# Linear attention on one core: the order of the row normalisation and the rotary sums on VectorE

## The chip, the cores and the metric

The kernel runs on one core of a Trainium2 chip. The metric is the device time of one execution in microseconds. The kernel before took 2188.58 us (median of three runs, 2188.2 to 2190.31 us).

## The reference, cut to what matters

The reference is a block of three layers over x of shape (2, 2048, 256) in f32: softmax attention, linear attention, and a feed-forward net of coupled cycles that stands between the two and again behind them. The change touches the linear attention alone. For each batch it computes:

```
q = silu(x @ Wq);  k = silu(x @ Wk);  v = x @ Wv      # 16 heads of 16
q = rope(q);  k = rope(k)        # t * cos + rotated(t) * sin
energy = (q @ k.T) * lower_triangle
out = energy @ v
out = out * sigmoid(x @ Wg1 @ Wg2)
mu = mean(out);  var = mean((out - mu) ** 2)
out = (out - mu) / sqrt(var + 1e-5) * ln_w + ln_b
x = x + out @ Wo
```

## The kernel before, in words

The five engines run programs of their own and meet at semaphores (names such as `l_s`, `l_n`; a wait names the count it wants). The linear attention goes over 32 tiles of 128 tokens (16 to a batch). The causal sum over earlier tiles is carried in a state (`s_x`, 256 x 16 values of k.T @ v laid on a diagonal), so each tile needs its own 128 x 128 energies and the state of the tile before.

`through_tiles` calls an engine's `pipeline(n, p, place)` for n = 0 to 33 in order; p is n's parity and picks one of two buffers. Tiles 4 to 13 and 18 to 29 are visited in two hardware loops, two tiles to an iteration (5 and 6 iterations, so 4 and 5 jumps back); the others are written out. One visit n works on several tiles at once. On TensorE, in this order, with the lines of the matmuls:

- `energy(n)` L860, sixteen matmuls of 32 rows, q.T k for tile n; `rows(n-1)` L892, the attention output of tile n-1 turned back into rows
- `project_vg(n+1)` L840 (values and gate), `project_qk(n+2)` L831 (queries and keys), `turn(n+1)` L848 (rotated q and k turned)
- `attend(n)`: L873 (state times q), L879 (masked energies times v), and at its end L883, which multiplies the rotated keys `qk_r` by v into the next state and then raises `l_s`
- `out_proj(n-2)` L910, and last `norm_turn(n-1)` L900: two transposes of the normalised rows `o_n` of tile n-1, behind `l_n`

On VectorE a visit is `mask(n, 0..3)` L1457 with `gated(n-1)` L1475 and L1478 (gate, then row statistics) between the masks, `variance(n-1)` L1481 and L1483, `rope(n+2)`, `normalise(n-1)` L1488, `state(n)` L1468 and `residual(n-2)` L1493. `rope` is four products of q and k with cosines and sines into a buffer `rt` (L1445) and then a difference and a sum (L1450, L1451, the sums from here on) into `qk_r[p]`. The sums wait for `l_s` of tile n: `qk_r` has two buffers, and the one for tile n+2 is still read by L883 of tile n. `normalise(n-1)` waits for `l_rs`, the reciprocal root that GpSimd makes (`output_root`, L1622) from the variance, and for `l_y` of the tile before. ScalarE takes the silu (L1120), copies results out of PSUM (`turned`, L1135 to L1141; the attention output, L1162) and applies the layer norm's weights to the turned rows (`affine`, L1148).

In a visit n the tiles for which a step has nothing to do leave it out: `normalise` and `norm_turn` are there from n = 1 on, `rope` up to n = 29. The order on each engine is written by hand; nothing reorders it.

Of the kernel before, what the change touches and what calls it, by code (L numbers as in the profile page):

```python
# [67 lines left out]
def hybrid_block(nc, x, wq, bq, wk, bk, wv, bv, wo, bo, lq, lk, lv, lo, g1, g2, ln_w, ln_b,  # L68
                 c1, d1, c2, d2, c3, d3, c4, d4, e1, f1, e2, f2, e3, f3, ar,
                 ident_in, cos_in, sin_in, causal_in, head_in, diag_in, sign_in, out):  # L70
    with ExitStack() as ctx:
# [112 lines left out]
        def take(*shape, dt=F32):  # L184
            n = int(np.prod(shape))
            words = n if dt == F32 else n // 2
            ap = work[:, at[0]:at[0] + words]
            at[0] += words
            assert at[0] <= WORK, at[0]
            if dt != F32:  # L190
                ap = ap.bitcast(dt)
            names = "abcd"[:len(shape)]
            return ap.rearrange(f"p ({' '.join(names)}) -> p {' '.join(names)}", **dict(zip(names, shape)))
# [33 lines left out]
        qk_a, qk_r = take(2, 2 * DIM), take(2, 2 * DIM)  # L227
# [92 lines left out]
        def is_tile(m):  # L320

            return not isinstance(m, int) or 0 <= m < TILES
# [17 lines left out]
        def wait(eng, s, value):  # L340

            if not isinstance(value, int) or value > 0:
                eng.wait_ge(s, value)
# [841 lines left out]
        def _(dve):  # L1185
# [5 lines left out]
            def moments_of(st, c):  # L1191

                g = st * NCH + c
                wait(dve, n_mv, g - 1)
                for t in range(4):
                    m = dve.bn_stats(bn6[:, c % 2, t], X[:, 4 * c + t, :])
                m.then_inc(n_bn, 1)
                dve.wait_ge(n_bn, g + 1)
                wait(dve, n_rs, g - NCH + 1)
                if st == 3:  # L1200
                    dve.wait_ge(n_sh, c + 1)
                for t in range(4):
                    m = dve.bn_aggr(moments[:, c, t], bn6[:, c % 2, t])
                m.then_inc(n_mv, 1)
# [227 lines left out]
            def halves(ap):  # L1432
                v = ap.rearrange("p (h a e) -> p h a e", a=2, e=HD // 2)
                return v[:, :, 0, :], v[:, :, 1, :]

            def rope(n, p, t):

                dve.wait_ge(l_silu, n + 1)
                wait(dve, l_rope, n)
                a, b = halves(qk_a[:, p, :])  # L1440
                ra, rb = halves(qk_r[:, p, :])
                co = cos_s[:, bass.ds(t, 1), :].broadcast_to((P, 2 * HEADS, HD // 2))
                si = sin_s[:, bass.ds(t, 1), :].broadcast_to((P, 2 * HEADS, HD // 2))
                for i, (u, v) in enumerate(((a, co), (b, si), (b, co), (a, si))):
                    m = dve.tensor_tensor(rt[:, i], u, v, ALU.mult)  # L1445
                m.then_inc(l_rt, 1)
                dve.wait_ge(l_rt, n + 1)
                wait(dve, l_s, n - 1)
                wait(dve, l_t, n - 1)
                dve.tensor_tensor(ra, rt[:, 0], rt[:, 1], ALU.subtract)  # L1450
                dve.tensor_tensor(rb, rt[:, 2], rt[:, 3], ALU.add).then_inc(l_rope, 1)  # L1451

            def mask(n, i):
                dve.wait_ge(l_e, 4 * (n + 1))
                if i == 0:
                    wait(dve, l_o, n)
                dve.tensor_tensor(e_m[:, i], ps[:, 3 + i, :].rearrange("p (a n) -> p a n", n=P),  # L1457
                                  causal[:].rearrange("p (a n) -> p a n", a=1).broadcast_to((P, 2 * KT, P)),
                                  ALU.mult).then_inc(l_em, 1)

            def state(n, reset):

                dve.wait_ge(l_s, n + 1)
                dve.wait_ge(l_o, n + 1)
                if reset:
                    dve.memset(s_x, 0.0).then_inc(l_sx, 1)
                else:
                    dve.tensor_tensor(s_x.rearrange("p k n -> p (k n)"), ps[:, 2, 0:DIM],  # L1468
                                      diag[:].rearrange("p h d -> p (h d)"), ALU.mult).then_inc(l_sx, 1)

            def gated(n, p):

                dve.wait_ge(l_gate, n + 1)
                dve.wait_ge(l_ot, n + 1)
                dve.scalar_tensor_tensor(out=o_r[:, p, :], in0=gate[:, p, :], scalar=1.0, in1=ps[:, 0, 0:DIM],  # L1475
                                         op0=ALU.add, op1=ALU.mult).then_inc(l_r, 1)
                dve.wait_ge(l_r, n + 1)
                dve.bn_stats(stats[:], o_r[:, p, :]).then_inc(l_bn, 1)  # L1478

            def variance(n, p):  # L1480
                dve.bn_aggr(mv[:, p, :], stats[:]).then_inc(l_mv, 1)  # L1481
                dve.wait_ge(l_mv, n + 1)
                dve.tensor_scalar(var_e[:, p:p + 1], mv[:, p, 1:2], EPS, None, ALU.add).then_inc(l_ve, 1)  # L1483

            def normalise(n, p):
                wait(dve, l_y, n - 1)
                dve.wait_ge(l_rs, n + 1)
                dve.tensor_scalar(o_n[:, p, :], o_r[:, p, :], mv[:, p, 0:1], rstd[:, p:p + 1],  # L1488
                                  ALU.subtract, ALU.mult).then_inc(l_n, 1)

            def residual(n):
                dve.wait_ge(l_w, n + 1)
                dve.tensor_tensor(X[:, bass.ds(n, 1), :], X[:, bass.ds(n, 1), :],  # L1493
                                  ps[:, 1, 0:DIM].rearrange("p (a n) -> p a n", a=1), ALU.add).then_inc(l_x, 1)

            def pipeline(n, p, place):
                if is_tile(n):
                    mask(n, 0)
                    mask(n, 1)
                if is_tile(n - 1):  # L1500
                    gated(n - 1, 1 - p)
                if is_tile(n):
                    mask(n, 2)
                if is_tile(n - 1):
                    dve.wait_ge(l_bn, n)
                if is_tile(n):
                    mask(n, 3)
                if is_tile(n - 1):
                    variance(n - 1, 1 - p)
                if is_tile(n + 2):  # L1510
                    rope(n + 2, p, place)
                if is_tile(n - 1):
                    normalise(n - 1, 1 - p)
                if is_tile(n) and is_tile(n + 1):
                    state(n, isinstance(n, int) and n % TPB == TPB - 1)
                if is_tile(n - 2):
                    residual(n - 2)
                if isinstance(n, int) and n >= TILES - 2:
                    for c in ((0,), (1,), (2, 3), (4, 5))[n - TILES + 2]:
                        dve.wait_ge(l_x, 4 * (c + 1))  # L1520
                        moments_of(3, c)

            dve.tensor_reduce(parity[:, 0:1], head[:].rearrange("p (j a) -> p a j", a=2)[:, 0:1, :], AX_X, ALU.add).then_inc(l_par, 1)
            dve.tensor_reduce(parity[:, 1:2], head[:].rearrange("p (j a) -> p a j", a=2)[:, 1:2, :], AX_X, ALU.add).then_inc(l_par, 1)
            dve.memset(v_x, 0.0).then_inc(l_vz, 1)
            rope(0, 0, 0)
            rope(1, 1, 1)
            dve.memset(s_x, 0.0).then_inc(l_sx, 1)
            through_tiles(dve, pipeline)

            dve.wait_ge(l_x, TILES)
# [164 lines left out]
```

## Time and profile before

| | |
|---|---|
| three runs, median (range) | 2188.58 us (2188.2 to 2190.31) |
| profiled execution | 2187.72 us |
| its span on the core | 2185.9 us |
| busy: TensorE, VectorE, ScalarE, GpSimd | 96%, 81%, 68%, 6% |
| mean granted TensorE clock | 0.979 |

The span is the time from the first to the last instruction that the profiler saw; the execution's own time has 1.82 us more around it. Granted clock 1.00 is 2.4 GHz and 0.50 is 1.2 GHz. Softmax attention fills the span to about 1400 us, the first feed-forward net to about 1685 us, the linear attention about 1685 to 1990 us, the second feed-forward net the rest.

### The profile page before, as it was taken

To read this page: it belongs to the slowest core of one execution; us is meant where nothing else is said; L and a number is where in the kernel's file an instruction comes from. 1 tells how busy PE (TensorE), PEld (TensorE's weight loads), DVE (VectorE), ACT (ScalarE), POOL (GpSimd) and SP (SyncE) were. 2 spreads that over 40 slices of the span, in tenths; PEclk is the share of its full clock that TensorE was granted. 3 is DMA by queue.
4 is the path that set the end of the run, shared out by engine and by line. 5 is a ranking of instruction groups with operands and counts; after the bars stand their busy time and mean duration, and the time that the engine had idled before them with its cause. 6 is when DMAs were issued, how large, how long until landed. Compare 5 with 4: busy or idle time off the path is not lost.

```text
span 2185.9 us, 48580 instructions
## 1 busy us (share of the span) xinstructions
PE 2102.3 (96%) x14502; PEld 880.0 (40%) x14502; DVE 1774.6 (81%) x3326; ACT 1476.2 (68%) x2899; POOL 134.0 (6%) x210
## 2 busy tenths in 40 slices
PE   7799999999999999999999999899998999998998
PEld 4323333333333333333333333244336555554435
DVE  6789999999999999999999999653546777775344
ACT  3438888888888888888888888744556434346653
POOL 1340000000000000000000000010002000002000
PEclk9779999999999999999999999999999999998999
DMA  6421221221221221211211211230000000000002
GB/s 161 139 64 42 53 73 41 62 63 41 64 60 41 67 57 43 71 51 46 73 47 50 72 43 49 78 106 11 0 0 1 1 0 1 0 0 1 0 1 78
DMA packets 93689, 101.24 MB, mean 46 GB/s; under 512 B 35712, under 2 KB 74896, under 8 KB 93552
## 3 DMA queue, kind: packets, MB, share of 16 engines
q1 hardware_dynamic: 93552, 99.79, 16.3%
q8 instruction: 40, 0.66, 0.1%
q14 instruction: 97, 0.79, 0.1%
HBM read 78.72 MB, written 20.71 MB: 45 GB/s over the span
## 4 chain that ended last, share of the span: by engine, by line
PE 85%; DVE 4%; issue 4%; ACT 3%; SPq 3%; DMA 1%; ACTq 0%; POOL 0%; DVEq 0%; POOLq 0%
PE ps L617 22%; PE ps L592 14%; PE ps L640 10%; PE ps L646 10%; PE ps L752 8%; PE ps L760 4%; PE ps L831 2%; PE ps L840 2%; PE ps L860 2%; ACT YT L1019 1%; PE ps L606 1%; PE ps L773 1%; PE ps L879 1%; PE ps L821 1%; SPq L359 1%
## 5 line engine op out<-in xcount | busy, mean ns | idle before, releaser
L1305 DVE TENSOR_REDUCE mx<-ps 128x1 f32<-128x512 f32 x2048 | 1279.4, 683 | 20.7 <-PE ps L592 15.5
L1019 ACT ACTIVATE YT<-ps 128x512 f32<-128x512 f32 x2048 | 1058.0, 606 | 250.8 <-PE ps L646 250.7
L617 PE MATMUL ps<-YT,work 128*32 128x512 f32 x4096 | 546.1, 605 | 0.0
L592 PE MATMUL ps<-work 64*128 64x512 bf16 x2048 | 461.0, 389 | 12.5 <-DVE mx L1305 10.5
L640 PE MATMUL ps<-work 64*128 64x512 bf16 x2048 | 401.8, 378 | 1.7
L646 PE MATMUL ps<-work 34*128 34x512 bf16 x2048 | 398.4, 378 | 0.0
L592 PEld LDWEIGHTS ps<-work 64*128 64x128 bf16 x2048 | 144.6, 93 | 617.8 <-DVE mx L1305 544.8
L640 PEld LDWEIGHTS ps<-work 64*128 64x128 bf16 x2048 | 161.6, 94 | 106.1 <-ACT YT L1019 31.6
L752 PE MATMUL ps<-YT,c_s 128*128 128x512 f32 x384 | 180.4, 613 | 3.2 <-ACT work L1059 2.5
L617 PEld LDWEIGHTS ps<-YT,work 128*32 128x32 f32 x4096 | 80.7, 108 | 122.8 <-issue 86.9
L1059 ACT ACTIVATE work<-ps,bias 128x512 f32<-128x512 f32 x96 | 60.7, 683 | 90.4 <-PE ps L752 90.4
L646 PEld LDWEIGHTS ps<-work 34*128 34x128 bf16 x2048 | 101.0, 94 | 49.5 <-issue 1.3
L1457 DVE TENSOR_TENSOR work<-ps,causal 128x512 f32<-128x512 f32 x128 | 81.8, 682 | 37.0 <-PE ps L860 37.0
L752 PEld LDWEIGHTS ps<-YT,c_s 128*128 128x128 f32 x384 | 70.4, 193 | 94.7 <-issue 94.6
L1590 POOL COPY work<-vals 128x512 f32 (+1 forms) x32 | 19.6, 614 | 1191.8 <-PE ps L617 1191.7
L760 PE MATMUL ps<-work,c_s 128*128 128x512 f32 x192 | 90.2, 592 | 0.0
L1395 DVE TENSOR_TENSOR work<-work,YT 128x512 f32<-128x512 f32 x36 | 24.7, 687 | 68.6 <-ACT work L1083 68.5
L1148 ACT ACTIVATE work<-ps,bias 128x128 f32<-128x128 f32 x64 | 25.8, 453 | 59.5 <-PE ps L900 59.5
L1128 ACT ACTIVATE work<-ps 128x128 f32<-128x128 f32 x64 | 14.3, 275 | 76.2 <-PE ps L840 76.2
L831 PE MATMUL ps<-lqk_s,work 128*128 128x512 f32 x128 | 62.1, 607 | 1.9 <-ACT work L1120 1.9
L840 PE MATMUL ps<-lvg_s,work 128*128 128x512 f32 x128 | 60.3, 594 | 0.0
L1445 DVE TENSOR_TENSOR work<-work,cos_s 128x256 f32<-128x256 f32 x64 | 27.2, 425 | 35.5 <-ACT work L1120 35.5
(151 smaller groups left out, 1775.9 us busy)
## 6 DMA issues: line engine op xcount, KB each, us to landing
work<-k_scr SPq DMA_DIRECT2D x640, 64.0 KB, 2.1
work<-q_scr SPq DMA_DIRECT2D x640, 32.0 KB, 1.8
o_scr<-o_sb SPq DMA_DIRECT2D x32, 256.0 KB, 2.2
X<-in_L_attn_a_x_dram SPq DMA_DIRECT2D x8, 512.0 KB, 7.2
work<-negt SPq DMA_DIRECT2D x256, 1.0 KB
work<-o_scr SPq DMA_DIRECT2D x16, 256.0 KB
work<-inv_scr SPq DMA_DIRECT2D x16, 256.0 KB
out_dram<-X SPq DMA_DIRECT2D x16, 256.0 KB, 2.1
```

The source lines that it names most:

```text
L592: mm(ps[:, bank_of[x], :], qa[rows, p, jp, qt * P:(qt + 1) * P], ka[rows, p, kc_ * CH:(kc_ + 1) * CH], start=True, stop=True).then_inc(a_m ...
L617: m = mm(ps[32 * j:32 * j + 32, 7, :], vst[:, p, t, :], prob(GROUP * t + j), start=t == 0, stop=t == KTILES - 1)
L640: mm(ps[:, S_BANK + (u + g) % S_RING, :], kb[rows, p, t * P:(t + 1) * P], qb[rows, p, jp, :], start=True, stop=False)
L646: mm(ps[:, S_BANK + (u + g) % S_RING, :], kc[rows, p, t * P:(t + 1) * P], qc[rows, p, jp, :], start=False, stop=True).then_inc(qk_mm, 1)
L752: m = mm(ps[:, mt, :], c1_s[:, kt, mt * P:(mt + 1) * P], YT[:, kt, ch(c)], start=kt == 0, stop=kt == KT - 1)
L760: m = mm(ps[:, 2, :], c2_s[:, kt, :], h1[:, (c - 1) % 2, kt, :], start=kt == 0, stop=kt == KT - 1)
L831: m = mm(ps[:, 0, :], y_st8[:, p, kt, :], lqk_s[:, kt, :], start=kt == 0, stop=kt == KT - 1)
L840: m = mm(ps[:, 1, :], y_st8[:, p, kt, :], lvg_s[:, kt, :], start=kt == 0, stop=kt == KT - 1)
L1019: fn(prob(u), ps[:, S_BANK + u % S_RING, :], ACT.Exp, scale=HD ** -0.5).then_inc(exp_ok, 1)
L1059: m = fn(h1[:, c % 2, mt, :], ps[:, mt, :], ACT.Gelu, bias=bias[:, D1 + mt:D1 + mt + 1])
L1305: dve.tensor_reduce(mx[:, p, at_:at_ + 1], ps[:, bank_of[x], :], AX_X, ALU.max).then_inc(a_max, 1)
L1457: dve.tensor_tensor(e_m[:, i], ps[:, 3 + i, :].rearrange("p (a n) -> p a n", n=P), causal[:].rearrange("p (a n) -> p a n", a=1).broadcast_ ...
```

## The change

`rope` is cut into two functions, its four products and its two sums. In a visit, `normalise(n-1)` is issued behind the products of tile n+2 and ahead of its sums; before, it came behind the sums. The wait for the silu stays with the products; the waits for the products themselves, for `l_s` and for `l_t` go with the sums. Nothing is added or removed: the same instructions and waits are issued in another order on VectorE, and no other engine's program is touched.

```diff
-            def rope(n, p, t):
+            def rope_products(n, p, t):
 
                 dve.wait_ge(l_silu, n + 1)
                 wait(dve, l_rope, n)
                 a, b = halves(qk_a[:, p, :])
-                ra, rb = halves(qk_r[:, p, :])
...
                 for i, (u, v) in enumerate(((a, co), (b, si), (b, co), (a, si))):
                     m = dve.tensor_tensor(rt[:, i], u, v, ALU.mult)
                 m.then_inc(l_rt, 1)
+
+            def rope_sums(n, p):
+
+                ra, rb = halves(qk_r[:, p, :])
                 dve.wait_ge(l_rt, n + 1)
                 wait(dve, l_s, n - 1)
                 wait(dve, l_t, n - 1)
...
                 if is_tile(n + 2):
-                    rope(n + 2, p, place)
+                    rope_products(n + 2, p, place)
                 if is_tile(n - 1):
                     normalise(n - 1, 1 - p)
+                if is_tile(n + 2):
+                    rope_sums(n + 2, p)
                 if is_tile(n) and is_tile(n + 1):
                     state(n, isinstance(n, int) and n % TPB == TPB - 1)
...
-            rope(0, 0, 0)
-            rope(1, 1, 1)
+            for n in range(2):
+                rope_products(n, n, n)
+                rope_sums(n, n)
```

## Rows read from the trace of the kernel before

**Rows 1.** The page: busy time by engine.

```profile
PE 2102.3 (96%) x14502; PEld 880.0 (40%) x14502; DVE 1774.6 (81%) x3326; ACT 1476.2 (68%) x2899; POOL 134.0 (6%) x210
```

**Rows 2.** By stretch: busy PE, PEld, DVE, ACT, POOL; clock; DMA share; GB/s.

```profile
60.00:200.00 140.00, 125.24 (x628) 42.56 (x627) 123.51 (x208) 70.04 (x124) 42.26 (x19) 0.82 0.29 83
...
1690.00:1965.00 275.00, 261.37 (x2267) 159.67 (x2267) 196.37 (x502) 111.84 (x328) 25.81 (x58) 1.00 0.00 1
```

**Rows 3.** Who waited for whom on TensorE, 1685 to 1990 us.

```profile
PE ps L900 <- DVE work L1488: 13.8, 30, 2.2
PE ps L860 <- issue: 2.1, 9, 0.3
```

**Rows 4.** The chain that ended last, part of a tile: start, length, what.

```profile
1867.61 0.68 DVE work L1445 x2
1868.29 0.39 issue
```

**Rows 5.** Timeline, TensorE in one tile: start, length, engine, line.

```profile
1765.35 1.08 PE L879 MATMUL ps<-work 128*32 128x128 f32 x32
1766.36 0.71 PE L883 MATMUL ps<-work 128*128 128x128 f32 x4
1766.91 1.03 PE L910 MATMUL ps<-lo_s,work 128*128 128x256 f32 x4
1768.31 0.44 PE L900 MATMUL ps<-ident,work 128*128 128x128 f32 x2 [0.37 <-DVE work L1488]
1768.67 1.15 PE L860 MATMUL ps<-work 32*128 32x256 f32 x16
...
1770.03 1.88 PE L840 MATMUL ps<-lvg_s,work 128*128 128x512 f32 x4
1771.74 1.94 PE L831 MATMUL ps<-lqk_s,work 128*128 128x512 f32 x4
```

**Rows 6.** Timeline, VectorE and GpSimd in the same tile.

```profile
1764.44 0.54 POOL L1622 TENSOR_TENSOR rstd<-var_e,mhalf 128x1 f32<-128x1 f32 x1 [8.56 <-DVE var_e L1483]
...
1766.49 0.42 DVE L1445 TENSOR_TENSOR work<-work,sin_s 128x256 f32<-128x256 f32 x1
1767.16 0.42 DVE L1450 TENSOR_TENSOR work<-work 128x256 f32<-128x256 f32 x1 [0.26 <-DVE work L1445]
...
1767.84 0.41 DVE L1488 TENSOR_SCALAR work<-work,mv,rstd 128x256 f32<-128x256 f32 x1
...
1768.50 0.41 DVE L1493 TENSOR_TENSOR X<-X,ps 128x256 f32 x1
1769.96 1.29 DVE L1457 TENSOR_TENSOR work<-ps,causal 128x512 f32<-128x512 f32 x2 [1.05 <-PE ps L860]
1771.17 0.41 DVE L1475 SCALAR_TENSOR_TENSOR work<-work,ps 128x256 f32<-128x256 f32 x1
```

**Rows 7.** Timeline, TensorE in visit 30, which has no rotary products or sums.

```profile
1969.81 1.03 PE L910 MATMUL ps<-lo_s,work 128*128 128x256 f32 x4
1970.68 0.38 PE L900 MATMUL ps<-ident,work 128*128 128x128 f32 x2
1970.99 1.15 PE L860 MATMUL ps<-work 32*128 32x256 f32 x16
```

**Rows 8.** Timeline, visit 1, the first with a normalisation and without `out_proj`.

```profile
1701.29 0.42 DVE L1445 TENSOR_TENSOR work<-work,sin_s 128x256 f32<-128x256 f32 x1
...
1701.43 0.71 PE L883 MATMUL ps<-work 128*128 128x128 f32 x4
1703.38 0.44 PE L900 MATMUL ps<-ident,work 128*128 128x128 f32 x2 [1.24 <-DVE work L1488]
```

**Rows 9.** Timeline, TensorE where a loop jumps back.

```profile
1758.78 0.44 PE L900 MATMUL ps<-ident,work 128*128 128x128 f32 x2 [0.37 <-DVE work L1488]
1759.44 1.15 PE L860 MATMUL ps<-work 32*128 32x256 f32 x16 [0.23 <-issue]
```

**Rows 10.** Timeline, TensorE in visit 31, after the tiles touched.

```profile
1976.23 1.94 PE L879 MATMUL ps<-work 128*32 128x128 f32 x32 [3.28 <-DVE work L1457]
```

## The prediction

> **What bounds the kernel now.** I began with the page. TensorE is busy 96% of the span, VectorE 81% [rows 1]. Over the whole TensorE is the bound, but a change in the linear attention is worth what that stage allows, so the second view was the busy time by stretch: between 1690 and 1965 us TensorE is busy 261.37 of 275 us at clock 1.00, VectorE only 196.37 us, and the DMA share is nil [rows 2]. No throughput is missing there; TensorE stands still for 13.63 us in small gaps. The third view, who waited for whom, names them: most are the transposes of the normalised rows, L900, waiting for VectorE's normalisation, 13.8 us in 30 waits over the whole stage, and nine short ones are "issue" ahead of L860 [rows 3]. One of the 30 (2.2 us) lies in visit 32, beyond the change; the 29 others make 11.6 us, and 11.6 + 2.1 us of issue waits is the 13.6 us, to a tenth.
>
> The chain of waits shows how one such gap arises: two rotary products, a pause of 0.39 us that the view calls issue, the two sums, and the normalisation, from which TensorE goes on [rows 4]. What the pause is can be read from one tile's timeline. The last product starts at 1766.49 and ends at 1766.91, the first sum starts at 1767.16 [rows 6]. The view puts the pause down to the product, but L883 ended at 1766.36 + 0.71 = 1767.07 [rows 5], 0.09 us before the sum, and the sums wait for it (`l_s`). So the sums follow TensorE's L883, and the normalisation, which needs nothing from TensorE at that moment, queues behind them. TensorE meanwhile has only L910 to do before L900.
>
> **The change part by part.** No instruction is added or removed; I cost the move of one VectorE instruction past two.
>
> *VectorE.* Instructions whose waits are met follow each other at less than their length: from the normalisation to the residual, two steps on, it is 1768.50 - 1767.84 = 0.66, or 0.33 us each [rows 6]. The normalisation will start at 1766.49 + 0.33 = 1766.82 and end 0.41 later, at 1767.23. The first sum could follow at 1767.15, and L883 does not release it before 1767.16: it moves by nothing, or by up to 0.1 us where the normalisation's length counts in full. That would be free as well, since `turn` reads the sums only a visit later. State and residual come 0.33 us earlier than before, as one instruction fewer stands between the sums and them; the residual would start at 1768.17, 0.23 us after L910's end at 1767.94 [rows 5], which it waits for. GpSimd's root ends at 1764.44 + 0.54 = 1764.98 [rows 6], 1.8 us before the normalisation wants it, so that wait does not come to stand ahead of the sums as a stall.
>
> *TensorE.* How soon can L900 follow L910 when nothing holds it? Visit 30 has no rotary part and shows it: 1970.68 - 1969.81 = 0.87 us from start to start, and 0.31 us on to L860 [rows 7]. In the ordinary tile it is 1768.31 - 1766.91 = 1.40 us, then 0.36 us [rows 5]. The gain is therefore 0.53 us up to L900, not the 0.37 us that the row marks as idle, since consecutive matmuls start before the modelled end of the one in front. It needs the normalisation by 1766.91 + 0.87 = 1767.78; it ends at 1767.23, with 0.55 us to spare. Visits 2 to 29 are such tiles: 28 x 0.53 = 14.8 us. Visit 1 has no L910: L900 started 1703.38; the normalisation will end at 1701.29 + 0.33 + 0.41 = 1702.03, and with 0.05 us to react L900 starts at 1702.08 [rows 8]: 1.3 us.
>
> *The step from L900 to L860.* It was 0.36 us where 0.31 is possible; in 19 of the 28 tiles 0.05 to 0.06 us each, 1.1 us. The other nine are the jumps back of the two loops, with 0.66 us (1759.44 - 1758.78) and 0.23 us marked issue [rows 9]; the count of nine is that of the issue waits [rows 3]. Before, TensorE's sequencer passed the wait for the normalisation only when the matmul units were already idle, and then the jump was paid in the open. Now the wait is met 0.55 us before L910 is through, and a jump of about 0.3 us (0.66 - 0.36) fits into that. Ends: 0 if the jump restarts the flow of instructions whatever the lead, 9 x (0.66 - 0.31) = 3.2 us if it is hidden. I take 3.2, since the lead is the larger number. The Trainium skill (Advanced Engine Details and Errata, Sequencer and Instruction Queues, Engine Queue Depths) gives TensorE a queue of 64 entries, and its Control Flow Timing prices a compare-and-branch at about 108 ns. By that page the sequencer can work ahead and the jump is hidden, as taken; no row here shows a jump of this loop with the wait met early.
>
> *What is late next.* Counted from L883's start, the residual will end at 1768.17 + 0.41 - 1766.36 = 2.22 us. The new energies start at 0.55 + 0.87 + 0.31 = 1.73 (L910 starts 0.55 behind L883) and the masks 1.29 us after them (1769.96 - 1768.67), at 3.02 [rows 5, 6]: VectorE has 0.8 us to spare there. `project_vg` overwrites the bank that the residual reads and comes at 1.73 + 1.36 = 3.09 (L840 follows L860 by 1770.03 - 1768.67): 0.87 us to spare. The tightest link is within the visit: energies, masks, gate, L831. The gate ends at 1771.17 + 0.41 = 1771.58 and L831 starts at 1771.74 [rows 5, 6]. It hangs on the energies, moves with them, and costs nothing new. If one of these covers were gone, a tile would give back what it is short, up to the 0.58 us gained.
>
> *Sum.* 14.8 + 1.3 + 1.1 + 3.2 = 20.4 us. What follows is moved forward whole: the stage's last visits and the second feed-forward net start from TensorE's and VectorE's last tiles. The profiled execution took 2187.72 us (span 2185.9 and 1.82 around it); less 20.4 that is 2167.3. The median of the runs is 0.9 us above that execution, so I predict **2168.2 us**, 0.93% less.
>
> *The clock behind the stage.* In visit 31 TensorE stands for 3.28 us and L879 then takes 1.94 us [rows 10]; the same 32 matmuls take 1.08 us at clock 1.00 [rows 5], so this is about the 1.2 GHz level. The stop does not go away, but the moment at which the clock changes need not move with the work. These 32 matmuls alone lose 0.86 us; if the slow stretch covers three such groups more or less, that is 2.6 us either way, an estimate from the two rows. It is not in the sum and is in the range.
>
> **Rivals.**
>
> *The jump stays in the open.* Then 3.2 us are missing: 2171.4. For it: nine clean issue gaps [rows 3]; against it: the lead of 0.55 us.
>
> *Only what is marked idle comes back.* The waits sum to 11.6 us for the 29 tiles [rows 3], which gives 2177.0. The Trainium skill (Perfetto Trace Analysis, Tensor Engine Instruction) says that a matmul's recorded end is estimated from its size, not observed; by it the idle figure is a matter of the model and starts are the thing to count. The trace agrees: visit 30 starts L900 0.16 us before L910's recorded end [rows 7]. So this rival needs L900 to react more slowly than there.
>
> *Something else holds the tile.* If another link ended about when the normalisation did, the gain would be used up: 0.58 us a tile is all there is, and a link only 0.1 us shorter leaves 29 x 0.1 = 2.9 us, so 2184.8, within what counts as no change. For it: the gate leaves L831 only 0.16 us, and ScalarE's and VectorE's waits are all on TensorE, so their slack shows only from where TensorE is now. Against it: that link moves with the energies, the others have 0.8 us, and visit 30 runs this stretch freely [rows 7].
>
> *Slower: the clock falls and stays down.* The stop of visit 31 will lie some 20 us earlier, and the second feed-forward net behind it is 196 us long (from 1990 to 2185.9). The stretch from 60 to 200 us had a mean clock of 0.82 with TensorE busy 125.24 of 140 us [rows 2], so a mostly busy stretch can be held back that much. At 0.82 the net would take at least 0.18 x 196 = 35 us more: 2203. It decides from 20.4 us lost, which is 41 us of TensorE's time at 1.2 GHz instead of 2.4. Against it: this stage at 95% busy held 1.00 [rows 2], and a denser one has no reason to be given less.
>
> **How the numbers follow.** The forecast has a chance of 0.72, the open jump 0.12, the idle figure alone 0.08, another link 0.05, the fallen clock 0.03. A measurement of this kernel tells 0.2%, 4.4 us, from no change. The first three are all more than that on the fast side: 0.92 faster, and 0.01 of the fourth with them; 0.04 the same, 0.03 slower. The range goes from 2168.2 less a clock stretch of 3, 2165, to the open jump with a clock stretch lost, 2171.4 + 3, rounded to 2175.
>
> **What would show it right or wrong.** In the profile after, the normalisation starts about 0.33 us behind the last product and the first sum stays about 0.1 us behind L883's end; TensorE's L910 to L900 is 0.87 us in visits 2 to 29 and the waits for L1488 there are gone, leaving the late visits; L900 to L860 is 0.31 us, at the jumps too (0.66 there means the first rival). It would be wrong if L900 still waits for VectorE, if a new wait of TensorE for masks, gate or residual appears, if the root is named ahead of the normalisation in many tiles, or if a stretch behind 1960 us runs longer at 1.2 GHz.

## The result, and the profile after

| | before | after |
|---|---|---|
| median (range), four runs each | 2188.39 us (2184.05 to 2190.31) | 2165.52 us (2162.47 to 2169.16) |
| profiled execution, its span | 2187.72, 2185.9 us | 2169.16, 2167.4 us |

The ratio is 0.990, with a 95% interval of 0.9881 to 0.992. The changed kernel was timed twice more in other groups of runs: 0.9912 (0.9897 to 0.9927) and 0.9908 (0.9894 to 0.9922). The predicted 2168.2 us is 2.7 us above the median, inside the range of 2165 to 2175.

First the busy time by engine on the page, then by stretch (busy PE, PEld, DVE, ACT, POOL; clock; DMA share; GB/s), of the kernel after. They answer to [rows 1, 2]: in the stage TensorE is busy 259.90 of 260 us.

```profile
PE 2096.4 (97%) x14502; PEld 882.0 (41%) x14502; DVE 1773.9 (82%) x3326; ACT 1476.9 (68%) x2899; POOL 134.3 (6%) x210
```

```profile
1690.00:1950.00 260.00, 259.90 (x2296) 164.69 (x2297) 198.82 (x510) 114.10 (x335) 26.26 (x59) 1.00 0.00 1
```

Who waited for whom on TensorE, 1685 to 1990 us, after. Against [rows 3], the issue waits of L860 are gone and the normalisation (now L1491) is waited for once, in visit 32; the 3.8 us for the masks were there before as well:

```profile
PE ps L879 <- DVE work L1460: 3.8, 2, 3.3
PE ps L900 <- DVE work L1491: 2.1, 1, 2.1
```

The timeline after, visit 5, at whose end a loop jumps back; TensorE, then VectorE. Line numbers of VectorE have moved: L1444 is the products, L1491 the normalisation, L1453 the first sum.

```profile
1740.07 0.71 PE L883 MATMUL ps<-work 128*128 128x128 f32 x4
1740.62 1.03 PE L910 MATMUL ps<-lo_s,work 128*128 128x256 f32 x4
1741.49 0.38 PE L900 MATMUL ps<-ident,work 128*128 128x128 f32 x2
1741.80 1.15 PE L860 MATMUL ps<-work 32*128 32x256 f32 x16
...
1740.04 0.42 DVE L1444 TENSOR_TENSOR work<-work,sin_s 128x256 f32<-128x256 f32 x1
1740.37 0.40 DVE L1491 TENSOR_SCALAR work<-work,mv,rstd 128x256 f32<-128x256 f32 x1
1740.88 0.42 DVE L1453 TENSOR_TENSOR work<-work 128x256 f32<-128x256 f32 x1
```

The normalisation sits in the pause: 0.33 us behind the last product. The first sum still comes 0.10 us behind L883's end (1740.78). L910 to L900 is 0.87 us and L900 to L860 is 0.31 us across the jump; [rows 5] had 1.40 us and [rows 9] had 0.66 us.

In visit 1, which has no L910, L900 now starts 0.65 us behind L883:

```profile
1706.45 0.71 PE L883 MATMUL ps<-work 128*128 128x128 f32 x4
1707.10 0.44 PE L900 MATMUL ps<-ident,work 128*128 128x128 f32 x2
```

**Where the 18.5 us between the two profiled spans lie.** I cut each span at the start of the energies (L860) of visit 0 and of visit 31. What lies between them is called the stretch below; the part ahead ends at the first cut, the part behind starts at the second.

| us | before | after | difference |
|---|---|---|---|
| ahead of the stretch | 1687.36 | 1692.38 | +5.02 |
| the stretch | 283.63 | 263.04 | -20.59 |
| behind it | 214.91 | 211.98 | -2.93 |

Only the stretch holds changed instructions. It can be added up from the starts of its visits: L910 to L900 in visits 2 to 29 went from 1.40 to 0.865 us, 28 x 0.53 = 14.9; L883 to L900 in visit 1 went from 1.95 to 0.65, 1.3; L900 to L860 over visits 1 to 29 went from 13.6 to 9.1 in all, 4.4, of which 3.2 lie at the nine jumps. Together 20.6 us.

### The profile page after: what moved, and what is told of

The parts are those of the page before. It is cut to its first block, busy times and chain, and to the rows that moved or that the text cites. A ratio compares the mean times of both kernels' runs of the same rounds, so it can differ in the third digit from the quotient of the medians.

```text
span 2167.4 us, 48580 instructions
## 1 busy us (share of the span) xinstructions
PE 2096.4 (97%) x14502; PEld 882.0 (41%) x14502; DVE 1773.9 (82%) x3326; ACT 1476.9 (68%) x2899; POOL 134.3 (6%) x210
## 4 chain that ended last, share of the span: by engine, by line
PE 88%; ACT 3%; SPq 3%; issue 2%; DVE 2%; DMA 1%; ACTq 0%; POOL 0%; DVEq 0%; POOLq 0%
PE ps L617 22%; PE ps L592 14%; PE ps L640 10%; PE ps L646 10%; PE ps L752 8%; PE ps L760 4%; PE ps L831 2%; PE ps L840 2%; PE ps L860 2%; PE ps L879 2%; ACT YT L1019 2%; PE ps L606 1%; PE ps L910 1%; PE ps L773 1%; PE ps L821 1%
## 5 line engine op out<-in xcount | busy, mean ns | idle before, releaser
L752 PE MATMUL ps<-YT,c_s 128*128 128x512 f32 x384 | 178.2, 607 | 3.2 <-ACT work L1059 2.5
L752 PEld LDWEIGHTS ps<-YT,c_s 128*128 128x128 f32 x384 | 69.7, 191 | 92.9 <-issue 92.7
L831 PE MATMUL ps<-lqk_s,work 128*128 128x512 f32 x128 | 62.1, 607 | 1.9 <-ACT work L1120 1.9
L840 PE MATMUL ps<-lvg_s,work 128*128 128x512 f32 x128 | 60.3, 594 | 0.0
L1444 DVE TENSOR_TENSOR work<-work,cos_s 128x256 f32<-128x256 f32 x64 | 27.2, 425 | 35.5 <-ACT work L1120 35.5
L760 PEld LDWEIGHTS ps<-work,c_s 128*128 128x128 f32 x192 | 36.3, 190 | 45.1 <-issue 45.1
```

The costliest lines, as they stand in the source:

```text
L752: m = mm(ps[:, mt, :], c1_s[:, kt, mt * P:(mt + 1) * P], YT[:, kt, ch(c)], start=kt == 0, stop=kt == KT - 1)
L760: m = mm(ps[:, 2, :], c2_s[:, kt, :], h1[:, (c - 1) % 2, kt, :], start=kt == 0, stop=kt == KT - 1)
L831: m = mm(ps[:, 0, :], y_st8[:, p, kt, :], lqk_s[:, kt, :], start=kt == 0, stop=kt == KT - 1)
L840: m = mm(ps[:, 1, :], y_st8[:, p, kt, :], lvg_s[:, kt, :], start=kt == 0, stop=kt == KT - 1)
```

## The experiments

The profile of each kernel gives its stretch; the same kernel, profiled three times, gave 263.04, 263.05 and 263.05 us. So a few tenths can be told apart there, where the time of the whole kernel moves by several us from run to run.

### TensorE's state product moved forward, in the kernel before

```diff
                 for kt in range(KT):
                     mm(ps[:, 7, kt * P:(kt + 1) * P], s_x[:, kt, :], q_t[:, p, kt, :], ...
+                [the two L883 matmuls and their l_s]
                 pe.wait_ge(l_em, 4 * (n + 1))
                 [the L879 matmuls]
-                [the two L883 matmuls and their l_s]
```

> The order of VectorE is that of the kernel before; only TensorE's state product (L883) moves ahead of the masked energies times v (L879), so that it raises l_s about 1.0 us earlier. My theory (the pause ahead of the rotary sums is the wait for L883): the first sum follows the last product by 0.04 us instead of 0.24 to 0.53, the normalisation ends 0.33 us earlier in the mean, TensorE's wait for it shrinks from 0.37 to about 0.04 us a tile, and the stretch from the energies of visit 0 to those of visit 31 takes 274.0 us where it took 283.6 before and 263.0 after. The rival (the pause is the products' own latency, as the view of the chain puts it): the stretch stays at 283.6 us.

Measured: stretch 273.4 us, median 2177.76 us (ratio 0.9952, 0.9928 to 0.9975). The timeline of visit 7 (L876 is the state product here, L883 the masked energies times v):

```profile
1754.70 0.61 PE L876 MATMUL ps<-work 128*128 128x128 f32 x4
...
1756.25 1.13 PE L910 MATMUL ps<-lo_s,work 128*128 128x256 f32 x4
1757.36 0.44 PE L900 MATMUL ps<-ident,work 128*128 128x128 f32 x2
...
1755.77 0.42 DVE L1445 TENSOR_TENSOR work<-work,sin_s 128x256 f32<-128x256 f32 x1
1756.22 0.42 DVE L1450 TENSOR_TENSOR work<-work 128x256 f32<-128x256 f32 x1
```

The state product ends at 1755.31, before the last product, and the first sum follows that product's end (1756.19) by 0.03 us instead of 0.24 to 0.53. The pause was TensorE's L883, though the profile put it down to VectorE's own product. This gives back only half of the 20.6 us, since both sums still stand ahead of the normalisation: L910 to L900 is still 1.28 to 1.30 us in the even visits of the loops (seven of them marked with a wait of 0.15 to 0.17 us, where I had expected about 0.04) and 1.11 to 1.13 us in the odd ones, and the nine jumps are still open.

### The normalisation between the two sums

```diff
                 dve.tensor_tensor(ra, rt[:, 0], rt[:, 1], ALU.subtract)
+                normalise(n - 1, 1 - p)
                 dve.tensor_tensor(rb, rt[:, 2], rt[:, 3], ALU.add).then_inc(l_rope, 1)
```

> The changed kernel with the normalisation between the two rotary sums, so that one sum and not two stands behind L883 and ahead of it. My theory (TensorE waits for exactly what stands in front of the normalisation): L910 to L900 takes 1.05 us (before 1.40, after 0.87), the jumps of the loops are open again at 0.66 us because the wait is met late, and the stretch from visit 0 to visit 31 takes 273.5 us. A rival, that the jump is hidden whenever the wait is shorter than before, gives 270.4; one that only the marked idle counts gives 0.20 us of the 0.37 still there and 277.8.

Measured: stretch 273.96 us; L910 to L900 is 1.06 us in visits 2 to 29, L900 to L860 is 0.66 to 0.72 us at the nine jumps. Median 2176.34 us (ratio 0.9949, 0.992 to 0.9977). One sum out of TensorE's way gives 0.34 us of the 0.53; the second gives the other 0.19, after which TensorE's own work is the longer. The profile of this kernel, visit 5:

```profile
1736.85 1.03 PE L910 MATMUL ps<-lo_s,work 128*128 128x256 f32 x4
1737.92 0.44 PE L900 MATMUL ps<-ident,work 128*128 128x128 f32 x2
...
1737.11 0.43 DVE L1453 TENSOR_TENSOR work<-work 128x256 f32<-128x256 f32 x1 [0.42 <-DVE work L1444]
1737.45 0.41 DVE L1492 TENSOR_SCALAR work<-work,mv,rstd 128x256 f32<-128x256 f32 x1
```

L900 is still held by VectorE here (the normalisation ends at 1737.86), yet no idle time is printed at L900, because it starts 0.04 us past the modelled end of L910, 1737.88. The rivals that counted the marked idle fail on this, and the one that hid the jumps behind any shorter wait (270.4 us) fails on the nine open jumps.

### The kernel before without TensorE's jumps

```diff
-            through_tiles(pe, pipeline)
+            for n in range(TILES + 2):
+                pipeline(n, n % 2, 0)
```

> The kernel before with TensorE's two loops of the linear attention written out, so that TensorE has no jump back; the other engines keep theirs. If the nine issue gaps ahead of L860 are the jumps, L900 to L860 is 0.36 us everywhere and the stretch from visit 0 to visit 31 takes 280.9 us (283.6 less 9 x 0.30). If they are something else, such as VectorE's or ScalarE's jumps, it stays at 283.6. If TensorE pays for fetching a longer program, it is above 283.6.

Measured: stretch 280.92 us, median 2183.1 us (ratio 0.9977, 0.9966 to 0.9989). L900 to L860 is 0.36 or 0.37 us in all 29 visits, and of [rows 3] only the first line is left. Who waited for whom on TensorE in this kernel, and its visit 5:

```profile
PE ps L900 <- DVE work L1489: 11.6, 29, 1.2
```

```profile
1742.34 0.44 PE L900 MATMUL ps<-ident,work 128*128 128x128 f32 x2 [0.37 <-DVE work L1489]
1742.71 1.15 PE L860 MATMUL ps<-work 32*128 32x256 f32 x16
```

So the nine gaps were TensorE's own loops, 0.30 us each: the jump back together with the counts that a loop's waits take from registers, which writing it out removes as well.

### One and two idle products more ahead of the normalisation

```diff
                 m.then_inc(l_rt, 1)
+                for i in range(1):     # 2 in the second kernel
+                    dve.tensor_tensor(idle[:, i], a, co, ALU.mult)
```

> The changed kernel with one idle product of 0.33 us between the rotary products and the normalisation, its result not used. That leaves the normalisation 0.19 us ahead of L900 in even visits and 0.38 us in odd ones, behind which the jumps lie. If the jump is hidden by the lead and needs about 0.35 us of it, nothing is lost: 263.0 to 264 us. If the jump needs more lead than that, up to the 0.71 us that it had, the nine open up by up to 0.35 us each: up to 266.2. If VectorE has no room, 29 x 0.33: 272.6.

> The changed kernel with two idle products more on VectorE between the rotary products and the normalisation, 0.33 us each; their results are not used. The normalisation ended 0.52 us (even visits) and 0.71 us (odd visits) ahead of L900's start; 0.67 us more leaves it 0.15 us late in even visits and just in time in odd ones. My theory (the jump is hidden by the lead): even visits lose 0.15 to 0.25 us each, 14 of them 2.8 us, and the nine jumps, all behind odd visits, are open again with 0.30 us each, 2.7 us: the stretch takes 268.5 us against 263.0. If any wait met in time hides the jump, only the first part is lost: 265.8. If VectorE has no room at all, all 29 visits lose 0.67 us: 282.4.

Measured with one: stretch 263.75 us, L910 to L900 still 0.87 us everywhere, L900 to L860 0.34 to 0.37 us at the jumps and 0.31 us elsewhere in visits 2 to 29; median 2167.05 us of two runs. Of the 0.71 us lost 0.32 us lie in visit 1 and the rest at the jumps. Measured with two: stretch 270.42 us; median 2172.92 us (ratio 0.9926, 0.9903 to 0.9948). With one, the end of visit 5:

```profile
1737.54 0.41 DVE L1494 TENSOR_SCALAR work<-work,mv,rstd 128x256 f32<-128x256 f32 x1
...
1738.32 0.38 PE L901 MATMUL ps<-ident,work 128*128 128x128 f32 x2
1738.67 1.15 PE L861 MATMUL ps<-work 32*128 32x256 f32 x16
```

With two, visit 4 and then visit 5:

```profile
1727.15 1.03 PE L911 MATMUL ps<-lo_s,work 128*128 128x256 f32 x4
1728.21 0.44 PE L901 MATMUL ps<-ident,work 128*128 128x128 f32 x2
...
1735.96 1.03 PE L911 MATMUL ps<-lo_s,work 128*128 128x256 f32 x4
1736.84 0.44 PE L901 MATMUL ps<-ident,work 128*128 128x128 f32 x2
1737.51 1.15 PE L861 MATMUL ps<-work 32*128 32x256 f32 x16 [0.23 <-issue]
```

The even visit is late by 1.06 - 0.87 = 0.19 us. The odd one is late by only 0.01 us, but its jump is open again (0.67 us). That is the clearest sight of the second effect: a wait that is met just as the engine runs dry costs nothing itself and still exposes the 0.35 us behind it. With a lead of about 0.37 us (one product; the normalisation ends at 1737.95, L901 starts at 1738.32) 0.03 to 0.06 us of the jump show, with 0.71 us none. The second kernel lost 7.4 us where I expected 5.5. Only the eleven even visits inside the loops are late, not all fourteen, for 2.3 us. What I had left out is visit 1 (0.65 us), the other visits' L900 to L860, which went back to 0.37 us (1.0 us together), and the odd visits: their jumps cost 0.35 us and not 0.30, and the wait itself up to 0.04 us.

### The normalisation ahead of the products too

```diff
+                if is_tile(n - 1):
+                    normalise(n - 1, 1 - p)
                 if is_tile(n + 2):
                     rope_products(n + 2, p, place)
-                if is_tile(n - 1):
-                    normalise(n - 1, 1 - p)
```

> The changed kernel with the normalisation ahead of the rotary products too, right behind the variance. GpSimd's root ends some 0.5 us before the silu is ready, so the normalisation just fits in between and the products start up to 0.15 us later. My theory (TensorE is bound by its own work now; both ends of VectorE's chain have room): the stretch stays at 263.0 us to 0.2. The rival (a wait for the root in front of products and sums stalls VectorE and so TensorE): 0.1 to 0.6 us a visit, 266 to 280 us.

Measured: stretch 263.03 us, median 2165.24 us of two runs. VectorE in this kernel:

```profile
1734.91 0.41 DVE L1491 TENSOR_SCALAR work<-work,mv,rstd 128x256 f32<-128x256 f32 x1 [0.81 <-POOL rstd L1628]
1735.24 0.42 DVE L1444 TENSOR_TENSOR work<-work,cos_s 128x256 f32<-128x256 f32 x1
...
1736.10 0.71 PE L883 MATMUL ps<-work 128*128 128x128 f32 x4
1736.91 0.43 DVE L1453 TENSOR_TENSOR work<-work 128x256 f32<-128x256 f32 x1 [0.25 <-DVE work L1444]
```

The pause ahead of the first sum is back, 0.10 us behind L883's end (1736.81), now that nothing is issued into it. In this visit, 5, the normalisation starts 5.64 us behind the energies where it started 7.13 us behind them. A microsecond and a half more of lead buys nothing, and a wait for GpSimd's root ahead of all VectorE's rotary work costs nothing: apart from what the gate still holds (next section), TensorE is the bound of the stage.

### Three further moves, and one of them alone

```diff
                     mask(n, 0)
-                    mask(n, 1)
                 if is_tile(n - 1):
                     gated(n - 1, 1 - p)
                 if is_tile(n):
+                    mask(n, 1)
                     mask(n, 2)
```

That is the early gate. The kernel with three moves has also the state product of the first experiment, and in visit 31 the moments of the first four tiles behind the masks:

```diff
                     variance(n - 1, 1 - p)
+                if isinstance(n, int) and n == TILES - 1:
+                    dve.wait_ge(l_x, 4)
+                    moments_of(3, 0)
...
-                for c in {TILES - 3: (0,), TILES - 2: (1,)}.get(n, ()):   # GpSimd's roots
+                for c in {TILES - 2: (0, 1)}.get(n, ()):
```

> The changed kernel with three more moves of order: VectorE's gate ahead of the second mask, TensorE's state product ahead of the masked energies times v, and in visit 31 the moments of the first four tiles (1.7 us) behind the masks, with GpSimd's roots to match. If TensorE, now without a wait in the stage, is bound only by the gate in even visits (L840 to L831 took 1.80 us there and 1.72 in odd ones), the early gate gives 14 x 0.08, about 1.1 us: the stretch takes 261.9. The state product alone gives nothing there, since L910 then takes 0.97 us for 0.87. In visit 31 TensorE's wait for the masks begins with the state product done and ends 0.66 us earlier: 1.2 us off the part behind, and 3 us more if the clock then stays up. In all 2 to 5 us less than the changed kernel. The rival: the gate is not what delays L831, the stretch stays at 263.0, and the late moments push the turns of the next stage back by as much as the masks gain: no difference.

> The changed kernel with nothing but VectorE's gate ahead of the second mask. In the kernel with three moves the stretch from visit 0 to visit 31 took 260.4 us and the part behind it 211.6. My theory (the gate alone made the 2.7 us: it held L831 back in all visits, and the moved moments only traded one wait of TensorE for two others): the stretch takes 260.4 us here too, L840 to L831 is 1.72 us everywhere, and the part behind is 212 or 215 us as in the changed kernel. The rival (the state product's place gives part of it): 261 to 262 us.

> The kernel with three moves once more, beside the one with the early gate alone and the changed kernel. If the state product and the moments are worth nothing by themselves, its stretch takes 260.4 us, the part behind 211.6, and its median lies within 2 us of the early gate's. If they spare the part behind the stretch the slow clock, its part behind is 211.6 us where the early gate's is 215, and its median lies 3 us lower.

| kernel | median (range), us | ratio (95%) | stretch |
|---|---|---|---|
| three moves | 2160.8 (2160.16 to 2164.1) | 0.9878 (0.9862 to 0.9894) | 260.36 |
| three moves, again | 2159.9 (2158.89 to 2160.82) | 0.9864 (0.9848 to 0.988) | 260.40 |
| early gate alone | 2164.09 (2159.41 to 2167.75) | 0.9885 (0.9867 to 0.9903) | 260.44 |

The early gate alone makes 2.60 us in the stretch, all three moves 2.64 to 2.69. Visit 4 with the early gate alone, then visit 4 of the kernel after:

```profile
1724.49 1.88 PE L840 MATMUL ps<-lvg_s,work 128*128 128x512 f32 x4
1726.20 1.88 PE L831 MATMUL ps<-lqk_s,work 128*128 128x512 f32 x4
1727.92 0.60 PE L848 MATMUL ps<-ident,work 128*128 128x128 f32 x4
```

```profile
1725.94 1.88 PE L840 MATMUL ps<-lvg_s,work 128*128 128x512 f32 x4
1727.74 1.95 PE L831 MATMUL ps<-lqk_s,work 128*128 128x512 f32 x4
1729.53 0.60 PE L848 MATMUL ps<-ident,work 128*128 128x128 f32 x4
```

L840 to L831 to L848 takes 1.71 + 1.72 us against 1.80 + 1.79. I had expected the gate to hold the fourteen even visits alone, by 0.08 us; it held the eleven even ones inside the loops by 0.16 and all the others by 0.06 (1.78 against 1.72 from L831 to L848), without an idle time in any row of TensorE. Those eleven visits are the first of each iteration, and VectorE's first mask starts later in them, 1.38 us behind the energies in visit 4 and 1.29 us in visit 5 of the kernel after (energies at 1724.59 and 1733.24):

```profile
1725.97 1.29 DVE L1460 TENSOR_TENSOR work<-ps,causal 128x512 f32<-128x512 f32 x2 [0.89 <-PE ps L860]
1734.53 1.29 DVE L1460 TENSOR_TENSOR work<-ps,causal 128x512 f32<-128x512 f32 x2 [0.79 <-PE ps L860]
```

It is so too in the kernel whose TensorE loops are written out, so it isn't TensorE's loop; whether it is VectorE's own was not tested.

The three moves beat the early gate alone by 3.3 us (in another group of runs) and 4.2 us (in the same one) in the medians, with ranges that overlap. The stretch has no part in that, and neither have the parts behind it in the profiles (211.6 and 211.0 against 210.8 us); I had expected 212 or 215 us behind the early gate's stretch, and the two medians within 2 us unless it was 215. The cause is open.

### The changed kernel again, and what the rest of the time does

> The changed kernel once more, as the measure for the others of this group. The stretch from the energies of visit 0 to those of visit 31 takes 263.0 us again, to 0.1. The measured gain of the change (22.9 us between medians) is larger than the 20.6 us of that stretch. My theory: the remainder is chance, since the part ahead of the stretch varied by 5 us over the profiles so far (1686.7 to 1692.4) and the part behind it takes about 211 or about 215 us, by whether TensorE's clock falls to 1.2 GHz in one stretch more; so over many rounds the gain comes out between 19 and 22 us. The rival (the change also speeds up what follows) gives 23 us or more again and always the short part behind, 212 us.

> The changed kernel as the measure on the same chip: 263.0 us for the stretch, 212 or 215.9 us behind it, the median 2.7 us above the early gate's.

Measured: medians 2169.21 us (2167.62 to 2169.76) and 2168.23 us (2167.1 to 2170.42), against 2187.72 and 2188.4 us of the kernel before in the same groups. The three groups put the gain at 22.9, 18.5 and 20.2 us, 20.5 us in the mean, beside the stretch's 20.6. The early gate's median lies 4.1 us below the changed kernel's in the same group, where I had expected 2.7. The rival of a speed-up behind the stretch is refuted: one of the three profiles has the longest part behind of all. This is what the profiles say of the two outer parts, with the mean granted clock of the 30 us from the second cut on:

| kernel | ahead | stretch | behind | clock |
|---|---|---|---|---|
| before | 1687.4 | 283.63 | 214.9 | 0.77 |
| after, three times | 1692.4, 1688.5, 1690.3 | 263.04, 263.05, 263.05 | 212.0, 215.9, 212.0 | 0.89, 0.77, 0.89 |
| state product | 1688.6 | 273.40 | 211.3 | 0.94 |
| between the sums | 1686.9 | 273.96 | 214.8 | 0.77 |
| no jumps | 1689.6 | 280.92 | 210.8 | 0.94 |
| one idle product | 1688.9 | 263.75 | 210.8 | 0.94 |
| two idle products | 1686.7 | 270.42 | 214.9 | 0.77 |
| ahead of products | 1688.4 | 263.03 | 211.9 | 0.89 |
| early gate | 1691.0 | 260.44 | 210.8 | 0.94 |
| three moves, twice | 1688.3, 1687.5 | 260.36, 260.40 | 211.6, 211.0 | 0.94, 0.94 |

The clock's three rows by stretch, from about the second cut on, of the kernel after in its second run, in its third, and of the early gate:

```profile
1952.00:1982.00 30.00, 21.64 (x111) 13.52 (x108) 23.05 (x84) 15.71 (x32) 13.17 (x34) 0.77 0.00 1
```

```profile
1953.00:1983.00 30.00, 22.17 (x123) 14.32 (x122) 23.65 (x85) 17.46 (x34) 13.12 (x34) 0.89 0.00 1
```

```profile
1951.00:1981.00 30.00, 21.65 (x131) 13.99 (x130) 23.65 (x85) 17.98 (x35) 13.12 (x34) 0.94 0.00 1
```

In the kernel after, the work of those 30 us waits five times, for 0.6 to 3.3 us, with the 3.28 us of visit 31 as the longest. The part behind is 215, 212 or 211 us as the mean clock there is 0.77, 0.89 or 0.94. The kernel after shows two of the three values with not one instruction different. The same matmuls in two of its executions. In the second run (first fence) L910 had a granted clock of 0.50 and L752 one of 0.58 in the mean, in the first run (second fence) both had 1.00:

```profile
1969.02 1.91 PE L910 MATMUL ps<-lo_s,work 128*128 128x256 f32 x4
1971.65 6.21 PE L752 MATMUL ps<-YT,c_s 128*128 128x512 f32 x8 [0.71 <-DVE X L1496]
```

```profile
1973.15 1.13 PE L910 MATMUL ps<-lo_s,work 128*128 128x256 f32 x4
1974.99 3.67 PE L752 MATMUL ps<-YT,c_s 128*128 128x512 f32 x8 [0.71 <-DVE X L1496]
```

The kernel with three moves waits 2.2 us in visit 31 instead of 3.28 and showed a mean clock of 0.94 both times. That would fit a schedule that gives the clock less cause to fall, but two profiles don't show it, and three other kernels (no jumps, one idle product, early gate) had 0.94 with the 3.28 us still there. At the same clock its part behind is no shorter than the early gate's: the moved moments came back as a wait of 3.0 us for ScalarE's `xn`, where the early gate's kernel waits 0.6 us, so the 1.2 us that I had expected there did not come and the rival was right about the moments.

## Why the prediction was right

- *The pause is L883, not the product.* Confirmed by the state product moved forward: with `l_s` early the pause is gone. With the normalisation ahead of the products it is back, again 0.10 us behind L883's end.
- *L910 to L900 gives 0.53 us, not the marked 0.37.* Measured 1.40 to 0.865 us in all 28 visits, 14.9 us against 14.8. Visit 30 of the kernel before [rows 7] was the right place to read the free pitch from: same instructions, without the part that the change moves.
- *Visit 1 gives 1.3 us.* Measured 1.3. It starts L900 0.65 us behind L883, as there is no L910.
- *L900 to L860: 1.1 and 3.2 us.* Measured 1.2 and 3.2. The jump was the one term with ends apart. That it is the loop's jump back is shown by the loops written out, that the lead hides it by the idle products. What I had not worked out is how much lead it takes: with 0.37 us, 0.03 to 0.06 us of it still showed. The Trainium skill (Advanced Engine Details and Errata, Engine Queue Depths) gives TensorE a queue of 64 entries, and the trace agrees with the reading that work can be taken in ahead: 0.31 us across the jump. The same page (Control Flow Timing) gives about 108 ns for one compare-and-branch, a third of the 0.30 us that a jump of this loop cost in the open; what makes up the rest was not taken apart.
- *Nothing new is late.* The masks wait for the energies with 0.79 us to spare where I had worked out 0.8.
- *The sum.* 20.4 us against 20.6 in the stretch. The profiled execution took 2169.16 us against the 2167.3 us worked out for it: 5.0 us more ahead of the stretch, 2.9 us less behind it. The second was in the range, as 2.6 us of clock; the first was not, and why the part ahead varies is open. The median lies 3.6 us below that execution, where I had added 0.9 us. As the stretch repeats, that too must lie in the parts that the change does not touch, but no profile shows the other executions. How close the median comes to the forecast is in part luck: the three groups gave 2165.52, 2169.21 and 2168.23 us.
- *The rivals.* The open jump, the marked idle and another link are refuted by L900 to L860 = 0.31 us, L910 to L900 = 0.87 us and the empty list of waits. The fallen clock did not come: the stage held 1.00 at 259.90 of 260 us busy, and the part behind took 212.0 to 215.9 us against 214.9 before. The time that I gave for another link, 2184.8 us, was 0.9 us too low: 2188.6 - 2.9 is 2185.7, since the other rivals count from the median.
- *One reading was too easy.* I called the link from the gate to L831 free because it moves with the energies. It costs nothing new, but it was never free: 2.6 us lay in it, in the spacing of matmuls of which none is marked idle.

## What to carry to other kernels

Where an engine waits for a result that itself waits for nothing recent, look at what stands ahead of it in its queue and what that in turn waits for: here one instruction of 0.33 us fitted into a pause of 0.24 to 0.53 us and took two others out of TensorE's way. Measure what a matmul can gain from start to start, against a visit of the same loop in which the wait is absent, not by the idle time printed at it. On TensorE here, a wait that was met 0.7 us before the engine ran dry also hid the loop's jump behind it; met just in time, it didn't.

## What the runs showed of the hardware that I had not expected

- A jump back of TensorE's loop cost 0.30 us in the open, 0.03 to 0.06 us with a lead of about 0.37 us, and nothing with 0.71 us.
- The same program's stage repeated to 0.01 us over three profiles, while 30 us behind it, with five stops of TensorE of 0.6 to 3.3 us, came out with a mean clock of 0.77 or 0.89 and 4 us apart. What decides between these is open.
- With `l_s` early, the first sum followed the end of the product that it needs by 0.03 us. The pause of 0.24 to 0.53 us in the kernel before, which the profile puts down to that product, was another engine's.
